# The full gelu of two layer-3 tiles written over its own PSUM bank, in a Macaron block with a recurrent middle

## The reference

```
def ffn(x):                                    # ternary weights, a scale per output
    h = silu(tlin(x, w1)) * tlin(x, w2)        # 128 -> 512     layer 1
    h = gelu(tlin(h, h1))                      # 512 -> 512     layer 2
    h = gelu(tlin(h, h2))                      # 512 -> 512     layer 3
    return tlin(h, w3)                         # 512 -> 128     layer 4

def mixer(x):
    xB = x @ B                                 # 128 -> 16
    h_t = tanh(xB_t + h_{t-1} @ A.T)           # along the 512 positions
    return (h @ C) @ W_out.T + b_out

x = x + 0.5 * ffn(layernorm(x))
x = x + mixer(layernorm(x))
x = x + 0.5 * ffn(layernorm(x))
```

## Time and profile before

| what | value |
|---|---|
| median of 3 runs | 433.95 us (432.31 to 434.37) |
| the profiled execution's own time | 432.54 us |
| its span | 430.7 us |
| mean granted clock of TensorE | 0.989 |
| TensorE busy | 391.6 us, 91% |
| VectorE busy | 323.5 us, 75% |
| ScalarE busy | 248.4 us, 58% |
| GpSimd busy | 165.5 us, 38% |

### The profile page before, as it was taken

The page is one execution under the profiler, slowest core; times in us unless marked ns, Lnnn a source line. Parts: engine busy times, 40 slices in busy tenths (PEclk is TensorE's granted clock), DMA queues, the critical chain, the costliest instruction groups (busy, mean ns, idle before and its releaser), DMA issues.

```text
span 430.7 us, 6662 instructions
## 1 busy us (share of the span) xinstructions
PE 391.6 (91%) x1787; PEld 298.0 (69%) x1787; DVE 323.5 (75%) x774; ACT 248.4 (58%) x585; POOL 165.5 (38%) x150
## 2 busy tenths in 40 slices
PE   5868999899998989999999999999999999999980
PEld 3656777676776667776777767778677777767760
DVE  4788798898888988757778776959777695978411
ACT  4646465674656647565663757656564656646450
POOL 3335254454324544224453333535243343535120
PEclk9899999999999999999999999999999999999997
DMA  7900000000000000000101000010101000010001
GB/s 264 416 5 2 25 2 3 25 0 24 3 24 0 0 24 0 24 2 3 48 1 49 2 24 27 0 49 2 49 0 49 0 24 24 0 50 2 24 1 32
DMA packets 6078, 14.02 MB, mean 33 GB/s; under 512 B 1056, under 2 KB 1568, under 8 KB 5792
## 3 DMA queue, kind: packets, MB, share of 16 engines
q1 hardware_dynamic: 5040, 13.37, 8.0%
q10 hardware_dynamic: 1008, 0.29, 0.3%
HBM read 7.37 MB, written 2.10 MB: 22 GB/s over the span
## 4 chain that ended last, share of the span: by engine, by line
PE 49%; issue 20%; DVE 14%; POOL 7%; ACT 7%; DMA 1%; ACTq 0%; DVEq 0%; POOLq 0%
PE F L256 39%; PE FR L256 4%; POOL y_lo L1263 4%; ACT y_hi L1030 3%; DVE y_lo L697 3%; DVE u L670 2%; DVE xnt_f L658 2%; DVE y L680 2%; POOL rs_m L1258 1%; PE FR L284 1%; PE SC L389 1%; DVE xnt_m L658 1%; DVE st_m L630 1%; ACT y L1027 1%; PE SC L374 1%
## 5 line engine op out<-in xcount | busy, mean ns | idle before, releaser
L256 PE MATMUL F<-y_hi,w_hi 128*128 128x512 f32 x512 | 213.3, 417 | 12.9 <-DVE y_lo L697 8.0
L256 PE MATMUL F<-y_lo,w_hi 128*128 128x512 f32 x512 | 202.5, 395 | 0.0
L1263 POOL TENSOR_TENSOR y_lo<-y,y_hi 128x512 fp32r<-128x512 f32 x96 | 133.7, 1405 | 128.9 <-DVE y_hi L687 73.2
L256 PEld LDWEIGHTS F<-y_hi,w_hi 128*128 128x128 f32 x512 | 96.2, 188 | 45.5 <-ACT y_hi L1030 12.9
L697 DVE TENSOR_TENSOR y_lo<-y,y_hi 128x512 fp32r<-128x512 f32 x96 | 87.2, 914 | 42.9 <-ACT y_hi L1030 42.2
L256 PEld LDWEIGHTS F<-y_lo,w_hi 128*128 128x128 f32 x512 | 96.6, 189 | 17.2
L1027 ACT ACTIVATE y<-F,sc 128x512 f32<-128x512 f32 x112 | 76.6, 684 | 53.6 <-PE F L256 53.5
L1030 ACT ACTIVATE y_hi<-F,sc 128x512 fp32r<-128x512 f32 x112 | 76.4, 682 | 0.0
L1046 ACT ACTIVATE h<-SC 128x32 fp32r<-128x32 f32 x104 | 20.4, 197 | 83.0 <-PE SC L389 82.4
L256 PE MATMUL F<-xn_hi,w_hi 128*128 128x512 f32 x119 | 50.1, 421 | 3.9 <-POOL w_lo L1303 1.9
L1009 ACT ACTIVATE th<-F,s1h 128x512 f32<-128x512 f32 x61 | 41.9, 687 | 20.3 <-PE F L256 17.8
(11 more groups left out here) (121 smaller groups left out, 357.6 us busy)
## 6 DMA issues: line engine op xcount, KB each, us to landing
x_all<-in_xT SPq DMA_DIRECT2D x1, 2048.0 KB, 16.9
x_all<-x1c SPq DMA_DIRECT2D x8, 256.0 KB, 2.3
x_all<-lnin SPq DMA_DIRECT2D x8, 256.0 KB, 2.3
out<-outb SPq DMA_DIRECT2D x8, 256.0 KB, 2.1
x_all<-in_xtok SPq DMA_DIRECT2D x1, 1536.0 KB, 12.5
w_raw<-in_h1T SPq DMA_DIRECT2D x2, 512.0 KB, 7.4
w_raw<-in_h2T SPq DMA_DIRECT2D x2, 512.0 KB, 9.2
x_all<-in_xtok SPq DMA_DIRECT2D x2, 256.0 KB, 4.3
```

Source lines behind the costliest of these rows:

```text
L256: mm = nc.tensor.matmul(out, wtile(w, layer, k, m), y, start=first and i == 0, stop=last and i == len(pairs) - 1)
L1263: pool.tensor_tensor(y_lo[:, k, :], y[:, k, :], y_hi[:, k, :].bitcast(F32), ALU.subtract).then_inc(out_sem, 1)
```

## The change

For tiles 1 and 2 of layer 3, in every turn, ScalarE first writes the high part, then evaluates the gelu a second time and writes it over its own input in PSUM (`FR` and `F[4]`). VectorE takes the low part from that bank and from `y3_hi`. A new semaphore, `y3_bank_r`, tells VectorE that the bank is written. ScalarE waits for its own high part (`y3_hi_r`) before it overwrites the bank from which that high part was read. The waits of TensorE that guarded `FR` and `F[4]` against being written too early now wait for `y3_lo_dve`, since VectorE is now the last reader. Tiles 0 and 3 stay as they were.

```
+            def bank_low(g, k):
+                dve.wait_ge(y3_bank_r, 2 * g + k)
+                nc.vector.tensor_tensor(y3_lo[:, k, :], B3[k][:, :], y3_hi[:, k, :].bitcast(F32),
+                                        ALU.subtract).then_inc(y3_lo_dve, 1)
...
-                low(g, 1, y3_hi_r, y23, y3_hi, y3_lo, y3_lo_dve)
+                bank_low(g, 1)
...
-                low(g, 2, y3_hi_r, y23, y3_hi, y3_lo, y3_lo_dve)
+                bank_low(g, 2)
...
+            def gelu3_bank(g, m, between):
+                act.wait_ge(l3_mm, 4 * g + m + 1)
+                wait(act, l4_mm, g)
+                s = sc[:, 3 * KT + m:3 * KT + m + 1]
+                nc.scalar.activation(y3_hi[:, m, :], B3[m][:, :], ACT.Gelu, scale=s).then_inc(y3_hi_r, 1)
+                between()
+                act.wait_ge(y3_hi_r, 4 * g + m + 1)
+                nc.scalar.activation(B3[m][:, :], B3[m][:, :], ACT.Gelu, scale=s).then_inc(y3_bank_r, 1)
+
             def gelu3(g, m, between=lambda: None):
+                if m in (1, 2):
+                    gelu3_bank(g, m, between)
+                    return
```

On TensorE, in `front_tokens` and `to_features` (both write `FR`) and in `layer1` for tile 0 (writes `F[4]`):

```
-                wait(pe, y3_hi_r, 4 * g - 6)
+                wait(pe, y3_lo_dve, (KT - 1) * (g - 2) + 1)
...
-                    wait(pe, y3_hi_r, 4 * g - 5)
+                    wait(pe, y3_lo_dve, (KT - 1) * (g - 2) + 2)
```

More of the change, by code:

```diff
@@ L199, in build @@
         y3_hi_r = sem("y3_hi_r")
+        y3_bank_r = sem("y3_bank_r")
         y3_lo_dve = sem("y3_lo_dve")
@@ L304, in layer1 @@
                         wait(pe, y3_hi_r, 4 * g)
+                        wait(pe, y3_lo_dve, (KT - 1) * g)
                     if m == 2:
@@ L939, in _ @@
                 layer1(1, m)
-            low(0, 1, y3_hi_r, y23, y3_hi, y3_lo, y3_lo_dve)
-            low(0, 2, y3_hi_r, y23, y3_hi, y3_lo, y3_lo_dve)
+            bank_low(0, 1)
+            bank_low(0, 2)
             layer1(1, KT - 1)
```

## The result

The changed kernel took 430.3 us (median of 4 runs, 429.76 to 430.83), the kernel before 433.57 us beside it (4 runs, 432.31 to 434.37). The ratio is 0.9927 with a 95% interval of 0.9898 to 0.9957: faster by 0.73%. The profiled execution took 430.83 us with a span of 429.0 us, 1.71 us less than the one of before (432.54).

A forecast was written before the change was run, and what follows sets the result against it. TensorE, busy for 91% of the span, was taken as the bound, so only closing its gaps helps. 1.4 + 0.9 = 2.3 us off the 433.95 us median gave 431.6 us (-0.53%), range 429.8 to 434.2, the forecast's own 430.7 to 432.8.

The forecast's parts named there:

- rival 4: VectorE's earlier release helps a second scan step of each middle turn as much, another 1.4 us: 430.2 us; chance 0.03.
- middle turns: Three turns: shorter low part 1 frees the small subtraction, closing TensorE's 0.46 us scan-step gap, 1.4 us in all.
- early turns: Five turns: shorter low part 2 lets gate and low part 3 start earlier; layer 4's last pair gains 0.18 us, 0.9 together.
- Rival 2: Nothing moves: the gaps come back at the next thing that is late; 433.9 us; chance 0.07.
- the shorter low parts of GpSimd beside it wait for nobody: Said of GpSimd's low parts beside VectorE's: their becoming shorter was counted among the edits at nothing.
- Full turns: Six turns of the second pass: TensorE's 0.54 us gap hangs on tile 3 alone, so worth 0.
- ScalarE's wait on itself: Waiting for its own high part costs ScalarE lost overlap, 0.11 to 0.27 us, taken as 0.2 per tile.
- Rival 1: Only middle turns gain, as ScalarE's wait on itself costs over 0.4 us more than taken: 432.5 us; chance 0.17.
- The pass over the bank: ScalarE's second gelu, written over its own input in PSUM, was to keep its length of 0.68 us.
- Rival 3: Slower: gelu over its own input takes 1.37 us, turning from about 0.5 us more per pass: 436.7 us; chance 0.11.
- VectorE's operand in PSUM: The low part pays for its PSUM operand: 0.69 us against the least of 0.669, 0.02 us, inside the spare time.

The follow-up runs named there:

- raw_bank: Kernel before, but VectorE takes low parts 1 and 2 from the bank still holding layer 3's sums before the gelu (results not the network's): 431.13 us, ratio 0.9944.
- tile1_only: Kernel before with the bank form for tile 1 alone, tile 2 as before: 429.27 us, ratio 0.9911.
- tile2_only: Kernel before with the bank form for tile 2 alone: 432.08 us, ratio 0.9976.
- tile3_too: Changed kernel with the bank form for tile 3 as well: 431.99 us, ratio 0.9969 to the kernel before.
- extra_pass: Changed kernel with one more gelu, into the unused SBUF tile, before each write of the bank: 434.05 us, ratio 1.0019 to the kernel before.
- sbuf_order: Changed kernel, but the second gelu writes the SBUF tile and VectorE subtracts from there: 433.6 us, ratio 1.0004 to the kernel before.
- tile1_repeat: Kernel before with the bank form for tile 1 alone, run again with more rounds: 430.43 us, ratio 0.9934.

## Why the prediction was right, and where it was not

The time came within the range, 1.3 us below the forecast of 431.6. The change in the medians is 0.73%, beyond the 0.5% that I drew as a line, though its interval reaches to 0.43%. The median of 430.3 lies below the forecast's own range of 430.7 to 432.8 and beside rival 4's 430.2, but not for rival 4's reason: the middle turns gave 1.40 us and not 2.8. What brought it there lies outside of the turns (see the median, below). To the end the sum was 2.3 us predicted and 2.2 measured. That is closer than its terms deserve, for two misses cancelled by luck: 0.3 us more from the early turns and 0.4 us less from the full ones.

*Middle turns, 1.4 us.* Right in mechanism and size. The gap at the scan step is gone, the turns are 0.48, 0.51 and 0.41 us shorter where 0.46 was predicted, and tile 1 alone does it, as `raw_bank` does with VectorE's operand alone. Rival 2, a gap that comes back at the next late thing, didn't happen.

*Early turns, 0.9 us.* The chain that I read (low part 2, gate, low part 3, last pair) is real, and the 0.18 us went, with low part 3 bound by the high part of tile 3 at 122.50. The forecast's 122.56 is 122.42 in this trace, whose turn runs 0.14 us earlier by then (layer 3's last matmul at 120.72 in place of 120.86); the 0.08 us between are those of the split wait, and the spare time covered them. The term was mis-sized: 1.19 us in place of 0.9. In turn 3 the next turn's first matmul too comes 0.08 us sooner, which I hadn't looked at; the other early turns weren't taken apart. And one sentence failed: "the shorter low parts of GpSimd beside it wait for nobody". No instruction waits for them, but VectorE's low part 2 shares their time. `tile1_only` shows that their earlier end alone shortens low part 2 from 1.30 to 0.84 us and brings the whole early term. `tile2_only` has the same gain by the path of the prediction, so the two paths cover each other and the sum didn't change; the sentence would have misled anyone who had split the change by my terms, as it misled my own expectation of that run.

*Full turns, worth 0.* The argument held for what it looked at: tiles 1 and 2 don't move the gap. It overlooked that the edit moves a wait of tile 3. The step that failed is to take "tiles 0 and 3 stay as they were" from the source, where the order of ScalarE's instructions in that loop has a row `L54 REGISTER_ALU [waits l3_mm]` in another place. It cost 0.08 us of gap in each of the five turns of the loop, 0.36 us in all.

*ScalarE's wait on itself, 0.2 us per tile.* It measures 0.14 us (0.71 us from start to start against 0.57), inside the bounds of 0.11 and 0.27, and 0.12 net on the critical tile, as `tile3_too` shows. Rival 1 needed 0.6.

*The pass over the bank, 0.68 us.* It is 0.66. Rival 3 is out, and `extra_pass` shows the price at which it would have come true. The small pair of the earlier trace rows had the right sign for the large one. The cleanest measure is `sbuf_order`, in which the same pass behind the same wait writes SBUF: 687 ns there, 659 into the bank. The Trainium skill, "ScalarE: Activation LUTs", section "Step-by-step: what each stage is for", calls PSUM the faster destination, and these two agree with it.

*VectorE's operand in PSUM, 0.02 us.* The means are 678 and 691 ns, beside 687 for the 64 from SBUF in the same trace, so not even the 0.02 is seen. The rule of the Trainium skill, "VectorE: DVE Perf Modes", section on the TRN2 errata, that a PSUM source costs 62 cycles more (an estimated 65 ns), isn't borne out for this operation: none of it is seen, and the measurement decides.

*The median.* The change in the medians, 3.3 us, is 1.1 us more than the turns account for. The rest must lie outside of the stretch, and it is of the size of the scatter there. In the two profiled executions those parts were even longer in the changed kernel, 51.91 us against 51.53 ahead of the transposes and 9.2 against 9.1 behind the last write, so no trace shows where the medians' 1.1 us come from.

## What to carry to other kernels

A 128x512 subtraction on VectorE with both operands in SBUF, beside GpSimd at work in SBUF, slows both of them (up to 1.78 us in place of 0.69, and 4.43 us for three of GpSimd's in place of 3.98). Taking one operand from PSUM frees both. VectorE's high part of layer 1, a cast from SBUF to SBUF that the change doesn't touch, still shows the fight: 1.02 us beside GpSimd (at 194.58 in the changed kernel), 0.43 with GpSimd idle (at 121.97). So ask what the partner's earlier end does for the next operation before adding up tiles. Gains of such an edit need not be additive: find the one tile that stands ahead of a gap, and leave the others, above all the critical one, as they are. In a loop, compare the order of the instructions and their waits also for the tiles that the edit doesn't name: a wait split off ahead of a critical instruction cost 0.08 us each time here.

## What was not expected of the hardware

The scatter between executions of one kernel, some 2 to 3 us, is nearly all outside of the stretch, and the larger part of it ahead of the first transposes. From there to the end the stretch is 367.89 and 367.93 us in the two profiled executions of the changed kernel, and 367.42 and 367.40 in those with tile 1 alone, whose own times were 428.55 and 431.19 us; 2.3 of these 2.6 us are ahead of the transposes. The two of the changed kernel (430.83 and 430.24 us) differ by 0.05 us there and by 0.7 behind the last write. The start of the transposes varies: 50.77 us (`tile1_only`), 51.53 (before), 51.91 (changed), 53.07 (`tile1_repeat`). It goes with TensorE's granted clock in the first 52 us, here a mean over stretches at its two levels, 2.4 and 1.2 GHz. The windows of that stretch (length, busy us and count of PE, PEld, DVE, ACT and POOL, granted clock, DMA share, GB/s) for the kernel with tile 1 alone:

```profile
0.00:52.00 52.00, 41.22 (x165) 30.91 (x166) 37.62 (x103) 28.55 (x49) 20.45 (x21) 0.97 0.39 147
```

and for its repeat:

```profile
0.00:52.00 52.00, 42.72 (x153) 31.73 (x154) 36.23 (x99) 28.03 (x47) 20.23 (x21) 0.90 0.38 142
```

It is one and the same program: with a mean granted clock of 0.97 TensorE did 165 matmuls in 52 us, with 0.90 it did 153. The changed kernel had 0.93 there, the kernel before 0.97. Across the 13 traces the order of the starts follows that number: 50.77 to 51.53 us at 0.97 (three traces), 51.91 to 52.88 at 0.93 (seven), 53.07 to 53.68 at 0.90 (three). Which of the two drives the other isn't shown. What decides in a given run how long the clock stays low at the start was not tried.
